# Moving weight splits and routing operations in VectorE's order of a gated cross-attention and expert kernel

## The chip, the core and the metric

One core of one Trainium2 chip. The time is that of one execution on the device, in microseconds (us). The kernel is written instruction by instruction: each engine has a program of its own, in a fixed order, and the engines meet at semaphores.

## The reference, cut to what matters

4096 rows (64 sequences of 64) of 128 numbers go through a gated attention against a context of the same shape, and then through a layer of 8 experts of which each row uses one.

```
q, k, v = rope(LN(x) @ Wq.T + bq), rope(ctx @ Wk.T + bk), ctx @ Wv.T + bv      # 16 heads of 8
x = x + tanh(g_xattn) * (softmax(q k / sqrt(8)) v @ Wo.T + bo)
z = LN(x)
logits = z @ Wr + br                                                        # 128 to 8
idx, gate = argmax(logits), the largest of softmax(logits)
x = x + tanh(g_ffn) * gate * (gelu(z @ W1[idx] + b1[idx]) @ W2[idx] + b2[idx])
```

## The kernel before

A tile is 128 rows (two sequences), so there are T = 32 tiles. All engines run through the same numbered steps (`pipeline(step)`), and in step i each works on tiles of different ages: on VectorE the query scaling of tile i, the key copy of tile i - 1, the row maxima of tile i - 2, the normalised output of tile i - 5 and the sum with the residual of tile i - 6. Nothing schedules this: the order of an engine's work in a step is the order of the code in its function `step`.

The engines' shares in an attention step are these.

- TensorE: query products (L748), key and value products (L749, L750), transposes of the stacked halves (L763), weighted values (L775), transpose of the normalised output (L788), scores (L799), transposed scores less the maxima (L814, L817), transposes of the output (L825), output product (L830, L831), transpose of the maxima (L839).
- VectorE: reciprocal and normalised output (L1132, L1135), query scaling `qk` (L1161), sum with the residual `x_all` (L1167), key copy `kT` (L1177), statistics of a coming tile (L865, L867, up to step 23), row maxima `mx` (L1195), casts of the rotated queries and keys `stk` (L1212, L1213), statistics of the finished rows (L1218, L1220).
- ScalarE: exponent `pr` (L569), maxima copy (L575), key scaling (L589), query copy `qT` (L606), output copies `oT`, `onT` (L612, L617), value copies `vx` (L627).
- GpSimd: subtraction for the low halves `stk` (L507), scatter of routed rows (L493), and the rotation (rope) in three operations (L522, L524, L528), which needs the scaled queries and keys of the same step. VectorE's casts need the rotated ones.
- The DMA queue loads the key blocks that the scores read, and the experts' weights.

Between these stands work of two other kinds. **Weight splits:** `EXPERT_AT` is step 4 + 3e for expert e. Two steps after, VectorE takes the last row off the first layer's weights (L1145, `w_f<-w_f,w_r`, 128 x 512), then ScalarE casts them to 16 bits (L601, `w_h`), and a step later VectorE makes the low half from both (L1149, `w_l<-w_f,w_h`). There are 8 of each, in steps 6 to 28. **Routing:** the tiles are routed in 5 groups (`GROUPS`). A group whose last tile is finished in step n is at `GROUP_AT` n = 11, 19, 27, 33, 37. VectorE adds epsilon in step n, and then works on the group in steps n + 2 (`before`: scaled L960, logits L970, max L976), n + 3 (`after`: difference L982, candidate L988, first L996, one-hot L1002, part L1008, count L1015) and n + 4 (`third`: exponent sum L1045, place L1026, destination L1033, index L1039, reciprocal L1051, gate L1057). Between count and place TensorE makes the ranks of the rows (`rank_of`, L662 to L669), by sums of one-hot rows. For the first three groups they go into PSUM bank 6, beside the query product's output, and for the last two into bank 1; they are issued in step n + 4, ahead of the query product in the first three groups.

After the attention, from step F0 = 35 on, 39 tiles of sorted rows pass through the experts: normalised and transposed, first layer (L710 to L712), gelu, second layer (L726, L728), final sum `fin` (L1260) and a scatter to the output (L540).

The lines of VectorE's step that say which group is at which stage, and where the weights' turn comes:

```
before, after, third = (GROUP_AT.get(i - n) for n in (2, 3, 4))
if after is not None:
    route_dif(after)
if third is not None:
    route_sum(third)
if i - 2 in EXPERT_AT:
```

## Time and profile before

| | |
|---|---|
| median of 3 runs | 324.67 us (323.63 to 325.26) |
| the profiled execution | 324.98 us |
| its span, first to last instruction | 323.2 us |
| busy: TensorE, its weight loads | 247.2 us (76%), 204.9 us (63%) |
| busy: VectorE, ScalarE, GpSimd | 196.2 (61%), 158.0 (49%), 182.6 us (57%) |
| mean granted TensorE clock | 0.928 of 2.4 GHz |
| DMA | 26.64 MB, 82 GB/s |

The median is what counts. The profile comes from one execution, with a time stamp for each instruction, so durations and waits are read in that one. Idle time in brackets behind a row is that of the engine just before the instruction, with what ended it. A blocked instruction, which was issued but can't go on, shows as a long one and not as idle time.

### The profile page before, as it was taken

To read this page: it belongs to the slowest core of one execution; us is meant where nothing else is said; L and a number is where in the kernel's file an instruction comes from. 1 tells how busy PE (TensorE), PEld (TensorE's weight loads), DVE (VectorE), ACT (ScalarE), POOL (GpSimd) and SP (SyncE) were. 2 spreads that over 40 slices of the span, in tenths; PEclk is the share of its full clock that TensorE was granted. 3 is DMA by queue.
4 is the path that set the end of the run, shared out by engine and by line. 5 is a ranking of instruction groups with operands and counts; after the bars stand their busy time and mean duration, and the time that the engine had idled before them with its cause. 6 is when DMAs were issued, how large, how long until landed. Compare 5 with 4: busy or idle time off the path is not lost.

```text
span 323.2 us, 10769 instructions
## 1 busy us (share of the span) xinstructions
PE 247.2 (76%) x3593; PEld 204.9 (63%) x3593; DVE 196.2 (61%) x680; ACT 158.0 (49%) x481; POOL 182.6 (57%) x222
## 2 busy tenths in 40 slices
PE   1458898888898978788878537694559898998970
PEld 1246677676677756577656426593559697996960
DVE  5457787888988889877797506652723333243420
ACT  1244667677676847676766203431523343343420
POOL 6475647476577886687867750046254434353450
PEclk9999999999999999999999755967897999799996
DMA  7612646254636342515111212201232212111100
GB/s 223 187 20 37 180 107 181 61 163 123 160 88 157 101 123 44 126 40 139 35 38 39 63 54 60 52 21 62 61 95 64 77 57 61 43 53 44 33 26 0
DMA packets 58537, 26.64 MB, mean 82 GB/s; under 512 B 38608, under 2 KB 53989, under 8 KB 58484
## 3 DMA queue, kind: packets, MB, share of 16 engines
q1 hardware_dynamic: 55204, 20.15, 25.1%
q0 software_dynamic: 2272, 4.46, 4.3%
q10 hardware_dynamic: 1008, 1.34, 1.4%
q8 instruction: 31, 0.51, 0.6%
q14 instruction: 22, 0.18, 0.2%
HBM read 16.69 MB, written 5.51 MB: 69 GB/s over the span
## 4 chain that ended last, share of the span: by engine, by line
PE 33%; DVE 19%; POOL 19%; issue 14%; another core or an unknown queue 5%; ACT 3%; POOLq 2%; DMA 1%; SPq 0%; DVEq 0%; ACTq 0%
PE ps L728 12%; POOL rot L528 5%; POOL rot L522 5%; POOL rot_s L524 5%; PE ps L710 3%; PE ps L712 3%; PE ps L711 3%; PE ps L763 2%; DVE qk L1161 2%; POOLq L91 2%; DVE mx L1195 2%; POOL stk L507 2%; DVE stk L1212 2%; PE ps L775 2%
## 5 line engine op out<-in xcount | busy, mean ns | idle before, releaser
L540 POOL DMA_INDIRECT out<-fin,got x39 | 37.9, 972 | 50.5 <-DVE fin L1260 35.9
L1195 DVE TENSOR_REDUCE mx<-ps 128x16 f16<-128x1024 f32 x32 | 39.1, 1221 | 22.1 <-PE ps L799 11.5
L728 PE MATMUL ps<-w_f,hT 128*128 x312 | 49.0, 305 | 0.0
L1260 DVE SCALAR_TENSOR_TENSOR fin<-ps,got 128x128 f32<-128x128 f32 x39 | 13.7, 351 | 57.2 <-PE ps L728 38.6
L728 PEld LDWEIGHTS ps<-w_f,hT 128*128 128x128 f32 x312 | 42.0, 209 | 1.1 <-issue 0.2
L522 POOL TENSOR_TENSOR rot<-qk,cf 128x256 f32<-128x256 f32 x32 | 23.4, 731 | 31.0 <-ACT qk L589 22.5
L493 POOL DMA_INDIRECT rows<-x_all,dest_i x32 | 34.0, 1062 | 8.2 <-issue 5.1
L817 PE MATMUL ps<-qT,kbd 128*128 128x64 f16 x512 | 34.8, 196 | 3.8 <-issue 3.8
L638 ACT ACTIVATE hT<-ps 128x512 f32<-128x512 f32 x39 | 23.3, 598 | 29.3 <-PE ps L712 24.0
L814 PE MATMUL ps<-mxT,ch 128*128 128x128 f16 x256 | 34.7, 225 | 2.0 <-issue 2.0
L569 ACT ACTIVATE pr<-ps 128x1024 f32<-128x1024 f32 x32 | 32.8, 1024 | 4.2 <-PE ps L817 3.3
L817 PEld LDWEIGHTS ps<-qT,kbd 128*128 128x128 f16 x512 | 32.0, 100 | 3.5 <-issue 3.5
L763 PE MATMUL ps<-ch,stk 128*128 128x128 f16 x256 | 20.7, 227 | 15.1 <-POOL stk L507 13.5
L710 PE MATMUL ps<-gT,w_h 128*128 128x128 f16 x156 | 31.7, 233 | 0.0
L711 PE MATMUL ps<-gT,w_h 128*128 128x128 f16 x156 | 31.6, 232 | 0.0
L712 PE MATMUL ps<-gT,w_l 128*128 128x128 f16 x156 | 31.5, 232 | 0.0
L763 PEld LDWEIGHTS ps<-ch,stk 128*128 128x128 f16 x256 | 16.0, 101 | 24.4 <-issue 14.1
L814 PEld LDWEIGHTS ps<-mxT,ch 128*128 128x128 f16 x256 | 25.5, 100 | 9.3 <-issue 9.2
L585 ACT ACTIVATE x_all<-ps 128x8 f32<-128x8 f32 x32 | 5.7, 178 | 51.7 <-DVE qk L1161 49.9
L507 POOL TENSOR_TENSOR stk<-rot,stk 128x256 f16<-128x256 f32 x32 | 21.4, 669 | 16.4 <-DVE stk L1213 16.4
L580 ACT ACTIVATE gT<-ps 128x128 f16<-128x128 f32 x39 | 10.8, 277 | 37.5 <-PE ps L697 24.0
L627 ACT ACTIVATE vx<-ps 64x64 f32<-64x64 f32 x128 | 27.9, 218 | 2.3
(160 smaller groups left out, 638.9 us busy)
## 6 DMA issues: line engine op xcount, KB each, us to landing
kbd<-kT SPq DMA_DIRECT2D x128, 32.0 KB
got<-rows SPq DMA_DIRECT2D x39, 72.0 KB
w_f<-in_W_rows SPq DMA_DIRECT2D x8, 256.0 KB, 2.9
w_r<-in_W_last_row SPq DMA_DIRECT2D x8, 256.0 KB, 3.1
w_f<-in_L_ffn_W SPq DMA_DIRECT2D x8, 256.0 KB
x_all<-in_x SPq DMA_DIRECT2D x3, 512.0 KB, 4.7
xt_all<-in_x_t SPq DMA_DIRECT2D x3, 512.0 KB, 4.4
ct_all<-in_ctx SPq DMA_DIRECT2D x3, 512.0 KB, 4.4
```

What stands on the lines that cost most here:

```text
L493: pool.indirect_dma_start(out=rows, out_offset=bass.IndirectOffsetOnAxis(ap=dest_i[:, t:t + 1], axis=0), in_=x_all[:, t, :], in_offset=Non ...
L522: pool.tensor_tensor(rot[:, par, :].rearrange("p (h d) -> p h d", d=HD), f, over_h(cos_t, 2 * H), ALU.mult).then_inc(rope1, 1)
L540: pool.indirect_dma_start(out=out_d, out_offset=bass.IndirectOffsetOnAxis(ap=got_i[:, u % GOT, R_ID:R_ID + 1], axis=0), in_=fin[:, u % FRI ...
L569: act.activation(pr[:, t % 2, :, :, :].rearrange("p j b q -> p (j b q)"), ps_st[:, :], ACT.Exp, scale=SCALE).then_inc(p_rdy, 1)
L710: pe.matmul(o, w_h, gT[:, par, 0, :], start=True, stop=False)
L711: pe.matmul(o, w_h, gT[:, par, 1, :], start=False, stop=False)
L712: mm = pe.matmul(o, w_l, gT[:, par, 0, :], start=False, stop=True)
L728: mm = pe.matmul(o, hT[:, par, c, :], w2_f[:, bass.ds(e, 1), c, :].rearrange("p o n -> p (o n)"), start=False, stop=(c == FC - 1))
L763: mm = pe.transpose(ps_stk[:, c:c + P], stk[:, par, first + a * P:first + a * P + P], ident_h)
L814: pe.matmul(ps_st[:, P * j:P * j + P], sel_h[:, j, :], mxT[:, par, :], start=True, stop=False)
L817: mm = pe.matmul(ps_st[:, c:c + S], kbd[:, s, j % 2, 2 * (j // 2) + b, :, :].rearrange("p h k -> p (h k)"), qT[:, s, j // 2, S * b:S * b + ...
L1195: dve.tensor_reduce(mx[:, t % 2, 0:H], ps_s[:, :].rearrange("p (h k) -> p h k", k=S), AX.X, ALU.max).then_inc(mx_done, 1)
```

## The change

VectorE's order in a step is written anew, and the ranks get another place. In words:

- The query scaling and the residual sum come right after the normalised output. The exponent sum, the two weight split operations and the place operation, which stood ahead of the query scaling, go behind it.
- Between the key copy and the row maxima now stand all of a group's operations of that step. The `before` stage has the difference in addition, so a group's difference is made one step earlier. The place operation alone stands ahead of the key copy. Nothing of the routing but the variance is left behind the maxima.
- The two weight splits stand between the key copy and the row maxima too.
- The ranks (`rank_of`) of all groups are made in step n + 3 instead of n + 4, after the transposes of the output, in bank 4, which the transpose of the normalised output and the output product use. They wait for the copy of that transpose. The next step's transpose into the bank waits until VectorE has read the ranks.

The order of GpSimd, ScalarE and of the DMA queue is the same.

```diff
-        ps_rank = [bank[6 if g <= EARLY else 1][:, 136:136 + 8 * NE] for g in range(len(GROUPS))]
-        ps_end = [bank[n][:, 208:208 + NE] for n in (6, 1)]
+        ps_rank = bank[4][:, 272:272 + 8 * NE]
+        ps_end = bank[4][:, 344:344 + NE]
...
@@ tensor, rank_of
-                if g > EARLY:
-                    pe.wait_ge(p_rdy, T)
-                    pe.wait_ge(g_read, g)
+                wait(pe, g_read, g)
...
@@ tensor, step
-                    if GROUP_AT.get(i - 4, len(GROUPS)) <= EARLY:
-                        rank_of(GROUP_AT[i - 4])
                     pe.matmul(ps_qx, xt_all[:, t, :], wqx[:, :], start=True, stop=True)
...
-                if GROUP_AT.get(i - 4, -1) > EARLY:
-                    rank_of(GROUP_AT[i - 4])
...
                     wait(pe, x2_done, t)
+                    if i - 4 in GROUP_AT:
+                        pe.wait_ge(g_read, GROUP_AT[i - 4] + 1)
                     pe.transpose(ps_onT, on[:, t % 2, :], ident).then_inc(onT_done, 1)
...
                     mm.then_inc(oT_done, 1)
+                if i - 3 in GROUP_AT:
+                    if live(i - 5):
+                        pe.wait_ge(onT_ev, i - 4)
+                    else:
+                        pe.wait_ge(x2_done, T)
+                    rank_of(GROUP_AT[i - 3])
...
@@ vector, step, after the normalised output
+                t = i
+                if live(t):
...
+                    dve.scalar_tensor_tensor(out=qk[:, t % 2, 0:D], in0=ps_q, scalar=rstd[:, t, :], in1=bq_bc[:, :],
+                                             op0=ALU.mult, op1=ALU.add).then_inc(qe_ev, 1)
+                t = i - 6
...
+                    dve.tensor_tensor(x_all[:, t, 0:QX], ps_op, x_all[:, t, 0:QX], ALU.add).then_inc(x2_done, 1)
+                if third is not None:
+                    route_place(third)
+                t = i - 1
...
+                    dve.tensor_copy(kT[:, t % 2, :, :].rearrange("p a n -> p (a n)"), ps_stk[:, NA * P:2 * NA * P]
+                                    ).then_inc(kT_ev, 1)
+                if before is not None:
+                    route_scaled(before)
                 if after is not None:
-                    route_dif(after)
+                    route_cand(after)
                 if third is not None:
                     route_sum(third)
+                    route_dest(third)
+                for t in STATS_AT.get(i, ()):
+                    stats_of(t)
+                if before is not None:
+                    route_logits(before)
+                if after is not None:
+                    route_first(after)
+                if third is not None:
+                    route_recip(third)
+                    route_index(third)
                 if i - 2 in EXPERT_AT:
...
                 if before is not None:
+                    route_max(before)
                 if after is not None:
                     route_onehot(after)
                 if third is not None:
+                    route_gates(third)
+                if before is not None:
+                    route_dif(before)
+                if after is not None:
+                    route_part(after)
+                    route_count(after)
                 t = i - 2
                 if live(t):
                     dve.wait_ge(s_done, t + 1)
                     wait(dve, mxT_done, t - 1)
                     dve.tensor_reduce(mx[:, t % 2, 0:H], ps_s[:, :].rearrange("p (h k) -> p h k", k=S), AX.X, ALU.max
                                       ).then_inc(mx_done, 1)
```

VectorE's order around the query scaling of step 12, before (`on` the normalised output, `w_f` the weights, `qk` the scaling, `kT` the key copy, `st`, `mv` the statistics, `mx` the maxima, `stk` the casts):

```order
L1135 TENSOR_TENSOR on<-ps,rden 128x128
L1145 TENSOR_TENSOR w_f<-w_f,w_r 128x512
L1161 SCALAR_TENSOR_TENSOR qk<-ps,rstd,bq_bc 128x128
L1167 TENSOR_TENSOR x_all<-ps,x_all 128x136
L1177 COPY kT<-ps 128x512
L865 BN_STATS st<-x_all 128x6
L867 BN_AGGR mv<-st 128x2
L1195 TENSOR_REDUCE mx<-ps 128x16
L1212 CAST stk<-rot 128x16x16
```

The same stretch now:

```order
L1137 TENSOR_TENSOR on<-ps,rden 128x128
L1147 SCALAR_TENSOR_TENSOR qk<-ps,rstd,bq_bc 128x128
L1153 TENSOR_TENSOR x_all<-ps,x_all 128x136
L1161 COPY kT<-ps 128x512
L867 BN_STATS st<-x_all 128x6
L869 BN_AGGR mv<-st 128x2
L1182 TENSOR_TENSOR w_f<-w_f,w_r 128x512
L1203 TENSOR_REDUCE mx<-ps 128x16
L1214 CAST stk<-rot 128x16x16
```

The subtraction `w_f` moved from ahead of the scaling to just ahead of the maxima. The low half `w_l` does the same in the steps that have it.

VectorE in step 13, where the first group is in its `before` stage and a low half is due, from the normalised output to the scaling of step 14, before:

```order
L1135 TENSOR_TENSOR on<-ps,rden 128x128
L1149 SCALAR_TENSOR_TENSOR w_l<-w_f,w_h 128x512
L1161 SCALAR_TENSOR_TENSOR qk<-ps,rstd,bq_bc 128x128
L1167 TENSOR_TENSOR x_all<-ps,x_all 128x136
L1177 COPY kT<-ps 128x512
L960 TENSOR_TENSOR logit<-x_all 128x48
L865 BN_STATS st<-x_all 128x6
L867 BN_AGGR mv<-st 128x2
L970 TENSOR_TENSOR logit<-logit,br_bc 128x48
L1195 TENSOR_REDUCE mx<-ps 128x16
L976 TENSOR_REDUCE lmax<-logit 128x6
```

Now:

```order
L1137 TENSOR_TENSOR on<-ps,rden 128x128
L1147 SCALAR_TENSOR_TENSOR qk<-ps,rstd,bq_bc 128x128
L1153 TENSOR_TENSOR x_all<-ps,x_all 128x136
L1161 COPY kT<-ps 128x512
L962 TENSOR_TENSOR logit<-x_all 128x48
L867 BN_STATS st<-x_all 128x6
L869 BN_AGGR mv<-st 128x2
L972 TENSOR_TENSOR logit<-logit,br_bc 128x48
L1186 SCALAR_TENSOR_TENSOR w_l<-w_f,w_h 128x512
L978 TENSOR_REDUCE lmax<-logit 128x6
L984 TENSOR_TENSOR ldif<-logit,lmax 128x48
L1203 TENSOR_REDUCE mx<-ps 128x16
```

The low half, the maximum of the logits and the difference (which stood in the next step, ahead of its scaling) are now ahead of the maxima.

TensorE at the end of step 14 and the start of step 15, before (`ps<-oh,ch` and `ps<-ohsum,ch` are the ranks, `wqx` the query product, `c_h` and `wo_x` the output product, `mx` the transpose of the maxima):

```order
L831 MATMUL ps<-wo_x,onT 128x136
L839 MATMUL ps<-ch,mx 128x128
L662 MATMUL ps<-oh,ch 128x48
L665 MATMUL ps<-oh,ch 128x40
L665 MATMUL ps<-oh,ch 128x32
L665 MATMUL ps<-oh,ch 128x24
L665 MATMUL ps<-oh,ch 128x16
L665 MATMUL ps<-oh,ch 128x8
L667 MATMUL ps<-ohsum,ch 128x48
L748 MATMUL ps<-wqx,xt_all 128x136
```

Now:

```order
L821 MATMUL ps<-cf,oT 128x128 x2
L660 MATMUL ps<-oh,ch 128x48
L663 MATMUL ps<-oh,ch 128x40
L663 MATMUL ps<-oh,ch 128x32
L663 MATMUL ps<-oh,ch 128x24
L663 MATMUL ps<-oh,ch 128x16
L663 MATMUL ps<-oh,ch 128x8
L665 MATMUL ps<-ohsum,ch 128x48
L832 MATMUL ps<-c_h,ch 128x136
L833 MATMUL ps<-wo_x,onT 128x136
L841 MATMUL ps<-ch,mx 128x128
L744 MATMUL ps<-wqx,xt_all 128x136
```

The ranks moved from between the transpose of the maxima and the query product to ahead of the output product of the step before.

## Rows read from the trace of the kernel before

**Rows 1.** The chain of waits, its shares of the span by line.

```profile
by line: issue 13.8%; PE ps L728 11.6%; another core or an unknown queue 5.2%; POOL rot L528 5.2%; POOL rot L522 5.2%; POOL rot_s L524 4.9%; PE ps L710 3.1%; PE ps L712 2.8%; PE ps L711 2.7%; PE ps L763 2.0%; DVE qk L1161 1.9%; POOLq L91 1.
```

**Rows 2.** VectorE's query scaling as a line: duration ns min/median/max, first and last start.

```profile
L1161 DVE SCALAR_TENSOR_TENSOR qk<-ps,rstd,bq_bc x32: 337/344/352, 11.6 to 175.5; 128x128 f32<-128x128 f32 x32
```

**Rows 3.** Timeline, VectorE, steps 9 and 10: start, duration, operation, idle before.

```profile
57.97 0.34 DVE L1161 SCALAR_TENSOR_TENSOR qk<-ps,rstd,bq_bc 128x128 f32<-128x128 f32 x1
...
62.48 0.68 DVE L1149 SCALAR_TENSOR_TENSOR w_l<-w_f,w_h 128x512 f16<-128x512 f32 x1
63.08 0.34 DVE L1161 SCALAR_TENSOR_TENSOR qk<-ps,rstd,bq_bc 128x128 f32<-128x128 f32 x1
...
63.55 0.42 DVE L1177 COPY kT<-ps 128x512 f16<-128x512 f16 x1
...
64.20 0.18 DVE L867 BATCH_NORM_AGGREGATE mv<-st 128x2 f32<-128x6 f32 x1
64.68 1.23 DVE L1195 TENSOR_REDUCE mx<-ps 128x16 f16<-128x1024 f32 x1 [0.30 <-PE ps L799]
66.28 0.29 DVE L1212 CAST stk<-rot 128x256 f16<-128x256 f32 x1 [0.38 <-POOL rot L528]
...
67.59 0.34 DVE L1161 SCALAR_TENSOR_TENSOR qk<-ps,rstd,bq_bc 128x128 f32<-128x128 f32 x1
```

**Rows 4.** Timeline, GpSimd, step 10: the three rotations.

```profile
64.03 0.72 POOL L522 TENSOR_TENSOR rot<-qk,cf 128x256 f32<-128x256 f32 x1 [1.61 <-ACT qk L589]
64.71 0.72 POOL L524 TENSOR_TENSOR rot_s<-qk,cf 128x256 f32<-128x256 f32 x1
65.52 0.73 POOL L528 TENSOR_TENSOR rot<-rot,rot_s 128x256 f32<-128x256 f32 x1
```

**Rows 5.** Timeline, TensorE, steps 9 and 10: products for the next step.

```profile
61.20 0.50 PE L748 MATMUL ps<-wqx,xt_all 128*128 128x136 f32 x2
...
61.97 0.22 PE L750 MATMUL ps<-bk_h,ch 128*128 128x128 f16 x1
...
66.14 0.45 PE L748 MATMUL ps<-wqx,xt_all 128*128 128x136 f32 x2
```

**Rows 6.** Timeline, ScalarE, step 9: weight cast and value copies.

```profile
58.78 0.63 ACT L601 ACTIVATE w_h<-w_f 128x512 f16<-128x512 f32 x1
...
60.20 0.95 ACT L627 ACTIVATE vx<-ps 64x64 f32<-64x64 f32 x4
```

**Rows 7.** VectorE beside GpSimd: timeline of steps 5 and 14, then a line's durations (ns).

```profile
41.23 0.67 POOL L507 TENSOR_TENSOR stk<-rot,stk 128x256 f16<-128x256 f32 x1 [0.61 <-DVE stk L1213]
41.56 0.89 DVE L1145 TENSOR_TENSOR w_f<-w_f,w_r 128x512 f32<-128x512 f32 x1
84.08 0.73 POOL L522 TENSOR_TENSOR rot<-qk,cf 128x256 f32<-128x256 f32 x1 [1.13 <-ACT qk L589]
84.58 0.29 DVE L1002 TENSOR_TENSOR oh<-cand,cmax 128x48 f16<-128x48 f32 x1
L1002 DVE TENSOR_TENSOR oh<-cand,cmax x5: 191/291/657, 84.6 to 223.3; 128x48 f16<-128x48 f32 x2, 128x64 f16<-128x64 f32 x2, 128x32 f16<-128x32 f32 x1
```

**Rows 8.** The row scatter as a line: duration ns min/median/max.

```profile
L493 POOL DMA_INDIRECT rows<-x_all,dest_i x32: 969/970/1467, 94.3 to 237.9; - x32
```

**Rows 9.** Timeline, VectorE: logit scaling of step 29, and scalings of steps 13 and 14.

```profile
164.17 1.69 DVE L960 TENSOR_TENSOR logit<-x_all 128x64 f32<-128x64 f32 x1
...
78.50 0.34 DVE L1161 SCALAR_TENSOR_TENSOR qk<-ps,rstd,bq_bc 128x128 f32<-128x128 f32 x1
...
83.14 0.34 DVE L1161 SCALAR_TENSOR_TENSOR qk<-ps,rstd,bq_bc 128x128 f32<-128x128 f32 x1
```

**Rows 10.** Timeline, first group's ranks on TensorE, and the scaling behind them.

```profile
87.79 0.18 PE L662 MATMUL ps<-oh,ch 128*128 128x48 f16 x1 [1.06 <-DVE ohsum L1015]
...
89.09 0.34 DVE L1161 SCALAR_TENSOR_TENSOR qk<-ps,rstd,bq_bc 128x128 f32<-128x128 f32 x1
```

**Rows 11.** Timeline, VectorE, the longest wait behind the last attention step.

```profile
193.41 1.22 DVE L1195 TENSOR_REDUCE mx<-ps 128x16 f16<-128x1024 f32 x1 [10.53 <-remote]
```

More of the change, by code:

```diff
@@ L668, in rank_of @@
                 if g in (EARLY, len(GROUPS) - 1):
[L669 removed]
+                    mm = pe.matmul(ps_end, ones_h, ohsum[:, g + 1, :], start=True, stop=True)
                 mm.then_inc(g_rank, 1)
@@ L1137, in step @@
                                       ALU.mult).then_inc(on_done, 1)
-                if after is not None:
-                    route_dif(after)
-                if third is not None:
-                    route_sum(third)
-                if i - 2 in EXPERT_AT:
-                    e = EXPERT_AT[i - 2]
-                    dve.wait_ge(s_w1ld[e % 2], 32 * (e // 2 + 1))
-                    dve.tensor_tensor(w1_f[:, e % 2, :], w1_f[:, e % 2, :], w1_r[:, e % 2, :], ALU.subtract).then_inc(s_w1c, 1)
-                if i - 3 in EXPERT_AT:
-                    e = EXPERT_AT[i - 3]
-                    dve.wait_ge(s_w1hi, e + 1)
-                    dve.scalar_tensor_tensor(out=w1_l[:, e, :], in0=w1_f[:, e % 2, :], scalar=W_SCALE,
-                                             in1=w1_h[:, e, :], op0=ALU.mult, op1=ALU.subtract).then_inc(s_w1lo, 1)
-                if third is not None:
-                    wait(dve, qkv_done, i + 1 if live(i) else 0)
-                    route_place(third)
                 t = i
@@ L1167, in step @@
                     dve.tensor_tensor(x_all[:, t, 0:QX], ps_op, x_all[:, t, 0:QX], ALU.add).then_inc(x2_done, 1)
-                if after is not None:
-                    route_cand(after)
                 if third is not None:
-                    route_dest(third)
+                    route_place(third)
                 t = i - 1
@@ L1181, in step @@
                 if after is not None:
-                    route_first(after)
+                    route_cand(after)
+                if third is not None:
+                    route_sum(third)
+                    route_dest(third)
                 for t in STATS_AT.get(i, ()):
@@ L1196, in step @@
                                       ).then_inc(mx_done, 1)
-                if before is not None:
-                    route_max(before)
-                if after is not None:
-                    route_part(after)
-                if third is not None:
-                    route_recip(third)
                 t = i
@@ L1238, in step @@
                     route_var(GROUP_AT[i])
-                if after is not None:
-                    route_count(after)
-                if third is not None:
-                    route_gates(third)
                 if i == F0 - 4:
```

19 lines of the change are left out of this document (13 added, 6 removed).

## The prediction

> **What bounds the kernel now.** I read the chain of waits first [rows 1]. Its largest named share is TensorE's second layer of the experts, which the change doesn't touch; then come GpSimd's three rotation operations, 5% of the span each. So the attention pipeline hangs on GpSimd, and on the small pieces of other engines between its turns. Then the query scaling of VectorE, which runs once a step [rows 2]: 32 times, from 11.6 to 175.5 us. The 31 steps between take 163.9 us, and the change lies almost wholly inside them. Below, q is the start of that operation, and times in a step are counted from it.
>
> A step without expert or routing work lasts 4.51 us, from 63.08 to 67.59 [rows 3]. In it the key copy begins at 0.47 and the statistics end at 1.30; the row maxima start at 1.60. GpSimd's rotations run from 0.95 to 1.67, 1.63 to 2.35 and 2.44 to 3.17 [rows 4]. VectorE waits 0.38 us for the last one, casts at 3.20, and reaches the next q 1.31 us after that. It idles 0.30 + 0.38 us between the key copy and the cast. That is the room into which the change moves work.
>
> Two more limits follow from the rows. From the start of the maxima, 64.68, to the first product of the next query, 66.14, are 1.46 us [rows 3, 5], and that group of products takes 0.99 (61.20 to 62.19) before q can start: a step lasts at least the start of the maxima plus 2.45. And the query product waits for ScalarE's value copies. With a weight cast, ScalarE takes 2.37 us from that cast, 58.78, to the end of the value copies, 61.15; the product starts 0.05 later [rows 5, 6].
>
> **The change part by part.**
>
> *Weight splits taken from ahead of q.* There are 16; one lasts 0.68 us and the next operation starts 0.60 after it did [rows 3]. The step from 57.97 to 63.08 has one ahead of its end and lasts 5.11 [rows 3]. Where VectorE's loop sets the step, each gives back 0.60.
>
> *Weight splits put beside the rotations.* In the new place a split is issued at about 1.33, within the rotation that runs from 0.95 to 1.67. VectorE operations that read two operands of SBUF do not run there. The one-hot comparison issued at 84.58 lasts 0.29, where 0.19 is its shortest, and ends 0.06 after the rotation [rows 7]. The first weight split met GpSimd's subtraction: it took 0.89 instead of 0.68 and ended 0.54 after the subtraction's end at 41.90 [rows 7]. The other way round, row scatters on GpSimd last 0.97 us and up to 1.47 [rows 8], and the long ones are those issued just after a split. So whoever comes first holds the other up, and a split needs 0.55 us in which GpSimd stands. The Trainium skill has this in "SBUF — State Buffer", section "Who interferes with whom": a VectorE instruction with two SBUF inputs contends with a GpSimd instruction that reads SBUF, and one of them blocks fully. The trace agrees, with the 0.89 above. By that rule the idle 0.68 us are no room for a split; taken as free room, they would give the faster rival's time below.
>
> No row has a weight split between two rotations, so I bound it. From below: it gets in when the first rotation ends, as five of the six small operations did that were waiting then (the bias addition twice, the one-hot comparison three times, at 0.29 to 0.66 us [rows 7]). From above: the logit scaling at 164.17 lasted 1.69, over two rotations [rows 9]. I take the first, as what most of the rows did, and keep the second.
>
> *A step with the low half:* split from 1.67 to 2.25, maxima from 2.25, the second and third rotation 0.6 later, cast at 3.81, next q at 5.12. It was 5.11. Nothing is gained.
>
> *A step with the subtraction of the last row:* the same on VectorE, but ScalarE's cast of these weights waits for it, and behind that cast stand the query copy, two output copies and the value copies. Before, the subtraction was done ahead of q. Now it ends at 2.30; the cast starts at 2.36, the value copies end at 4.73, the products run from 4.78 to 5.77: a step of 5.75 for 5.11, so +0.64.
>
> *Routing operations.* They take three steps for each of the groups in the attention: scaling, bias, maximum and difference in 13, 21, 29; candidate, maximum, comparison, part and count in 14, 22, 30; place, sums, reciprocal, index and gate in 15, 23, 31. All now stand ahead of the maxima, at 0.15 to 0.25 us each, and each with two SBUF inputs waits out a rotation. Step 13 lasted 4.63, from 78.50 to 83.14 [rows 9]. Now the bias addition ends with the first rotation, the low half gets in at 2.37 and ends at 2.97, the third rotation runs until 3.70, the difference waits for it, the maxima start at 3.78: 3.78 + 2.45 = 6.23, and only 0.60 comes back in the step before. In the same way step 14 gets 6.15 for 5.96, and step 15, where the subtraction slips to the second gap and ScalarE follows it, 6.47 for 5.25.
>
> *Ranks a step earlier, in the output product's bank.* TensorE idled 1.06 us for the count and began the ranks at 87.79, with the query products behind them, so that q came at 89.09 [rows 10]. Of that step's 5.96 the subtraction is 0.60 and the ranks about 0.35. Now they run while VectorE takes the maxima. In return the read of the ranks, 0.2 us, stands between the output sum and the key copy, and the transpose into the bank waits for it with the scores behind. The 0.30 of idle time ahead of the maxima hides that; uncovered it would be 0.2 in three steps.
>
> *The sum*, in threes of steps, worked by these rules for both kernels so that the same errors stand on both sides:
> steps 5 to 7: +1.55 (the first subtraction loses 0.42 ahead of q, but the key copy is late there and the split meets the second gap: 6.47 for 5.11);
> 8 to 10: +0.65, and 17 to 19: +0.70, the plain kind;
> 11 to 13, 14 to 16, 20 to 22, with group work: +1.55, +1.55, +1.15;
> 23 to 28: -0.05, since from 24 on there are no statistics, splits come before the first rotation, and the scatters, free of the 0.5 us that splits cost them, give back what the rotations lose;
> 29 and 30: -0.95, the ranks.
> Together +6.15. After the attention nothing changes its kind. The long wait of the maxima, 10.53 us until 193.41 [rows 11], lies behind nine row scatters that start from the last attention step, so I let it move with that step. The profiled execution becomes 324.98 + 6.15 = 331.1; it lies 0.31 above the median of 324.67, so the median should be **330.8**.
>
> **The rivals.**
>
> *The splits get in only in the second gap*, like the logit scaling [rows 9]. Maxima start at 2.97, the steps last 5.42 and 6.47 instead of 5.12 and 5.75: +1.02 in each plain triple, nothing where they are there already, +3.0 in all by the same rules: 333.8. For it: one waiting operation was passed over. Against it: five were not. If they are passed over until the third rotation ends, it is 342; no row shows that.
>
> *Faster: a long operation shares the port.* If a split runs its 0.68 us beside a rotation, as the statistics do [rows 3, 4], the maxima start at 1.93, under the 2.06 that a 4.51 us step allows. Each low half then gains 0.60, and each subtraction gains 0.60 ahead of q and costs 0.9 through ScalarE (1.99 + 0.06 + 2.37 + 0.05 + 0.99 = 5.46 for 4.51); with the ranks the rules give -2.65, so 322. It decides at a split of 0.68 beside rotations of 0.73. Against it stands the 0.89.
>
> *Little or no difference.* My three group triples stand on margins of 0.05 us between the issue of an operation and the end of a rotation; if they lose half, and late steps hide more, +1 to +2 is left.
>
> **How the numbers follow.** The forecast's case gets 0.52, its own range 328 to 333; the second gap 0.22 (332.5 to 336), the third 0.04; the faster rival 0.12 (320 to 323); little or none 0.10 (323.5 to 327). A measurement tells 0.5%, 1.6 us, from no change. Faster by more 0.12, within 0.07, slower 0.81. The range 326 to 336 leaves out the faster rival and the third gap.
>
> **What would show it.** In the changed kernel's trace: splits issued about 1.3 after q that last 0.9 to 1.0 us (second gap: 1.6), a second rotation of about 1.3 us; a step near 5.75 where ScalarE's weight cast starts with the end of the subtraction and TensorE waits for the value copies; step 13 over 6; scatters in the attention near 1.0; no idle time for the count ahead of the ranks; the last scaling at about 181.5 instead of 175.5. I am wrong if splits last 0.68 and rotations 0.73 there, or if the last scaling comes by 176, and wrong in size if the steps with group work last under 5.5.

## The result, and the profile after

| | before | after |
|---|---|---|
| median | 324.97 us (4 runs) | 335.44 us (4 runs, 334.62 to 336.48) |
| the profiled execution, its span | 324.98, 323.2 us | 335.75, 334.0 us |
| last query scaling, step 31 | 175.5 us | 186.9 us |
| from there to the end of the span | 147.7 us | 147.1 us |

The change makes the kernel slower: the ratio is 1.032 (95% interval 1.028 to 1.035). That is within the forecast range of 326 to 336, by 0.6 us, and 4.6 us above the 330.8 forecast: outside the 328 to 333 of the forecast's own case and inside the 332.5 to 336 of the rival with the second gap. Up to the last query scaling 11.4 us are lost, and 0.6 come back behind it.

From the page of the kernel after: the span, the busy times, and the chain that ended last, by line.

```profile
span 334.0 us, 10768 instructions
...
PE 253.3 (76%) x3593; PEld 204.5 (61%) x3593; DVE 208.2 (62%) x680; ACT 161.2 (48%) x481; POOL 187.0 (56%) x222
...
PE ps L726 9%; DVE mx L1203 4%; PE ps L759 3%; PE ps L708 3%; DVE w_f L1182 3%; DVE kT L1161 2%; PE ps L710 2%; PE ps L709 2%; POOL rot L528 2%; PE ps L745 2%; ACT vx L627 2%; POOL rot_s L524 2%; POOL rot L522 2%; ACT pr L569 2%
```

VectorE runs as many instructions as before and is busy 12.0 us longer (208.2 for 196.2), since operations that are issued and blocked count as busy. In the chain the rotations fell from 5% each [rows 1] to 2%. The subtraction `w_f` (L1182) is new in it, with the row maxima right behind it.

The subtraction (with who waited for it: us, times), the low half, GpSimd's second rotation and the scatter as lines of the kernel after: duration ns min/median/max, first and last start.

```profile
L1182 DVE TENSOR_TENSOR w_f<-w_f,w_r x8: 658/1129/2168, 43.4 to 163.2; 128x512 f32<-128x512 f32 x8
...
  ACT w_h L601: 14.6, 8
...
L1186 DVE SCALAR_TENSOR_TENSOR w_l<-w_f,w_h x8: 678/793/1198, 49.9 to 170.7; 128x512 f16<-128x512 f32 x8
...
L524 POOL TENSOR_TENSOR rot_s<-qk,cf x32: 718/728/1208, 13.2 to 188.7; 128x256 f32<-128x256 f32 x32
...
L493 POOL DMA_INDIRECT rows<-x_all,dest_i x32: 966/976/1187, 97.8 to 248.7; - x32
```

Splits last up to 2.17 us, and ScalarE's weight cast waits 14.6 us for the eight subtractions. The scatters behave as I wrote: 1.19 at most for 1.47 [rows 8]. So the scatters no longer lose time to splits, but nothing came back for it.

The plain step with a subtraction, step 9: timeline of the kernel after (start, duration, operation, idle before), VectorE, then GpSimd and ScalarE.

```profile
57.94 0.34 DVE L1147 SCALAR_TENSOR_TENSOR qk<-ps,rstd,bq_bc 128x128 f32<-128x128 f32 x1
...
59.15 1.00 DVE L1182 TENSOR_TENSOR w_f<-w_f,w_r 128x512 f32<-128x512 f32 x1
60.07 1.21 DVE L1203 TENSOR_REDUCE mx<-ps 128x16 f16<-128x1024 f32 x1
...
63.69 0.35 DVE L1147 SCALAR_TENSOR_TENSOR qk<-ps,rstd,bq_bc 128x128 f32<-128x128 f32 x1 [0.72 <-PE ps L746]
```

```profile
58.88 0.72 POOL L522 TENSOR_TENSOR rot<-qk,cf 128x256 f32<-128x256 f32 x1 [1.52 <-ACT qk L589]
59.56 1.17 POOL L524 TENSOR_TENSOR rot_s<-qk,cf 128x256 f32<-128x256 f32 x1
```

```profile
60.18 0.63 ACT L601 ACTIVATE w_h<-w_f 128x512 f16<-128x512 f32 x1 [1.27 <-DVE w_f L1182]
```

The split is issued 1.21 after q, lasts 1.00 instead of 0.68, and ends 0.55 after the first rotation; the second rotation lasts 1.17 instead of 0.72. ScalarE's cast starts with the split's end, and the next q waits 0.72 us for TensorE. The step is 63.69 - 57.94 = 5.75, for 5.11 before. This is the mechanism of the forecast, complete; that the number agrees to the hundredth is luck, as said further down.

Late in the attention it looks otherwise. Step 24, same views:

```profile
144.94 0.35 DVE L1147 SCALAR_TENSOR_TENSOR qk<-ps,rstd,bq_bc 128x128 f32<-128x128 f32 x1
...
145.95 2.17 DVE L1182 TENSOR_TENSOR w_f<-w_f,w_r 128x512 f32<-128x512 f32 x1
148.04 1.21 DVE L1203 TENSOR_REDUCE mx<-ps 128x16 f16<-128x1024 f32 x1
...
152.03 0.35 DVE L1147 SCALAR_TENSOR_TENSOR qk<-ps,rstd,bq_bc 128x128 f32<-128x128 f32 x1 [1.37 <-PE ps L746]
```

```profile
145.05 1.06 POOL L493 DMA_INDIRECT rows<-x_all,dest_i  x1 [0.19 <-POOL stk L507]
146.14 0.74 POOL L522 TENSOR_TENSOR rot<-qk,cf 128x256 f32<-128x256 f32 x1
146.82 0.73 POOL L524 TENSOR_TENSOR rot_s<-qk,cf 128x256 f32<-128x256 f32 x1
147.64 1.06 POOL L528 TENSOR_TENSOR rot<-rot,rot_s 128x256 f32<-128x256 f32 x1
```

```profile
148.15 0.63 ACT L601 ACTIVATE w_h<-w_f 128x512 f16<-128x512 f32 x1 [2.24 <-DVE w_f L1182]
```

The split was issued during a row scatter, 0.16 us before that ended. It stayed blocked through the first and the second rotation and ran in the second gap. ScalarE waited 2.24 us. The step lasts 7.09 for 5.21. Step 27 does the same (split 2.09, step 7.13 for 5.52).

There is a second loss in it. TensorE waited for ScalarE's output copy, and soon after its granted clock fell. TensorE in step 24, then two windows with their length, busy times and clock (the number before the DMA share):

```profile
149.59 0.44 PE L821 MATMUL ps<-cf,oT 128*128 128x128 f32 x2 [1.60 <-ACT oT L612]
...
150.91 0.91 PE L745 MATMUL ps<-wkv,ct_all 128*128 128x256 f32 x2
```

```profile
148.00:149.50 1.50, 0.00 (x0) 0.00 (x0) 1.50 (x4) 1.35 (x4) 0.70 (x1) 1.00 0.28 47
...
151.20:154.40 3.20, 3.14 (x46) 1.99 (x46) 1.77 (x4) 2.03 (x7) 1.79 (x3) 0.50 0.09 28
```

TensorE had nothing for 1.60 us; soon after, the clock stood at 0.50, its lower level of 1.2 GHz, for over 3 us, then came back. The key and value product took 0.91 there and takes 0.59 at full clock. By step the clock is 0.93, 0.78, 0.92 and 0.80 in steps 24, 25, 27 and 28, and 1.00 in every other step from 5 to 30. Before the change it is 1.00 in all of them. The Trainium skill ("TensorE: Matmul & The Clock Gate", Part 1) says that the clock has these two levels and falls after the engine has been idle; the trace agrees on the levels, with 0.50 and 1.00. That this wait brought the clock down is not shown: in the same kernel TensorE idled as long in steps 15 and 21, 1.53 and 1.66 us, and kept 1.00. In step 21:

```profile
130.60 0.44 PE L821 MATMUL ps<-cf,oT 128*128 128x128 f32 x2 [1.66 <-ACT oT L612]
```

Where the 11.4 us came from, in the triples of the forecast:

| steps | forecast | measured |
|---|---|---|
| 5 to 7 | +1.55 | +0.95 |
| 8 to 10 | +0.65 | +0.46 |
| 11 to 13 | +1.55 | +1.47 |
| 14 to 16 | +1.55 | +1.47 |
| 17 to 19 | +0.70 | +1.30 |
| 20 to 22 | +1.15 | +1.02 |
| 23 to 28 | -0.05 | **+4.98** |
| 29, 30 | -0.95 | -0.26 |
| sum | +6.15 | +11.39 |

The term of steps 23 to 28 was 5.0 us too low, of the 5.2 us that are missing. The others were off by up to 0.7 us each way and cancel to 0.2.

### The profile page after: what moved, and what is told of

The parts are those of the page before. It is cut to its first block, busy times and chain, and to the rows that moved or that the text cites. A ratio compares the mean times of both kernels' runs of the same rounds, so it can differ in the third digit from the quotient of the medians.

```text
span 334.0 us, 10768 instructions
## 1 busy us (share of the span) xinstructions
PE 253.3 (76%) x3593; PEld 204.5 (61%) x3593; DVE 208.2 (62%) x680; ACT 161.2 (48%) x481; POOL 187.0 (56%) x222
## 4 chain that ended last, share of the span: by engine, by line
PE 31%; DVE 26%; issue 13%; POOL 9%; another core or an unknown queue 8%; ACT 8%; DMA 1%; POOLq 0%; SPq 0%; DVEq 0%; ACTq 0%
PE ps L726 9%; DVE mx L1203 4%; PE ps L759 3%; PE ps L708 3%; DVE w_f L1182 3%; DVE kT L1161 2%; PE ps L710 2%; PE ps L709 2%; POOL rot L528 2%; PE ps L745 2%; ACT vx L627 2%; POOL rot_s L524 2%; POOL rot L522 2%; ACT pr L569 2%
## 5 line engine op out<-in xcount | busy, mean ns | idle before, releaser
L1203 DVE TENSOR_REDUCE mx<-ps 128x16 f16<-128x1024 f32 x32 | 38.9, 1217 | 18.5 <-remote 10.6
L726 PE MATMUL ps<-w_f,hT 128*128 x312 | 48.2, 302 | 0.0
L726 PEld LDWEIGHTS ps<-w_f,hT 128*128 128x128 f32 x312 | 41.2, 206 | 1.1 <-issue 0.2
L522 POOL TENSOR_TENSOR rot<-qk,cf 128x256 f32<-128x256 f32 x32 | 23.3, 729 | 28.2 <-ACT qk L589 20.1
L493 POOL DMA_INDIRECT rows<-x_all,dest_i x32 | 32.0, 1001 | 7.9 <-issue 5.5
L528 POOL TENSOR_TENSOR rot<-rot,rot_s 128x256 f32<-128x256 f32 x32 | 27.3, 854 | 2.5
L759 PE MATMUL ps<-ch,stk 128*128 128x128 f16 x256 | 21.5, 233 | 8.9 <-POOL stk L507 3.6
```

What stands on the lines that cost most here:

```text
L528: pool.tensor_tensor(rot[:, par, :], rot[:, par, :], rot_s[:, par, :], ALU.add).then_inc(rope_done, 1)
L726: mm = pe.matmul(o, hT[:, par, c, :], w2_f[:, bass.ds(e, 1), c, :].rearrange("p o n -> p (o n)"), start=False, stop=(c == FC - 1))
L759: mm = pe.transpose(ps_stk[:, c:c + P], stk[:, par, first + a * P:first + a * P + P], ident_h)
L1203: dve.tensor_reduce(mx[:, t % 2, 0:H], ps_s[:, :].rearrange("p (h k) -> p h k", k=S), AX.X, ALU.max).then_inc(mx_done, 1)
```

## The experiments

Most runs fell on chips where the kernel before takes 304.7 to 305.0 us and not 324.97; only the last experiment had 324.97 beside it. So I took the kernel before once more there, with its profile.

**before_again**: the kernel before, no edit.

> The kernel before, with a profile on this chip, to see where the 20 us between the chips lie. If they lie in the waits behind the attention (10.5 us of the maxima and two others of 5 and 6.4 us), the last query scaling starts at 175.5 as before and the rest is shorter; if the chip is faster throughout, every step is shorter.

Measured: 305.28 us, span 303.5. Its steps agree with those of the first profile to within 0.03 us, but for step 30 (6.15 for 6.24), and the last scaling is at 175.5 in both. The 20 us lie behind it. VectorE's waits in the first profile, then here (total, times, longest):

```profile
DVE fin L1260 <- remote: 14.0, 3, 6.4
...
DVE mx L1195 <- remote: 10.5, 1, 10.5
```

```profile
DVE fin L1260 <- PE ps L728: 44.9, 37, 2.5
DVE mx L1195 <- PE ps L799: 12.8, 21, 2.0
```

The waits put down to "remote", the 10.53 us of [rows 11] among them, don't exist on the other chips. The kernel after has them as well on the first chip, at 10.6 us for 10.5, so they are no matter of the change. I therefore read each experiment against the kernel before on its own chip, as a difference; expectations in absolute numbers near 325 mean that difference too.

**changed_again**: the changed kernel on such a chip.

> The changed kernel itself, beside the kernel before, on the chip of these studies, on which the kernel before takes 304.7 to 305.0 us instead of 324.97. If the loss lies in the attention steps alone, the difference is the same 10.5 us or a little more (11.4 by the last query scaling), so 315 to 317; if a part of it is due to the waits behind the attention, it differs by more than 2 us from that.

Measured: 316.21 for 305.03 us, +11.2, ratio 1.036 (1.030 to 1.042); last scaling at 187.1. Loss and step lengths are those of the first chip (steps to within 0.07 us), and so is the clock (0.94, 0.77, 0.92, 0.80 in steps 24, 25, 27, 28).

**splits_back**: the changed kernel with both weight splits ahead of the query scaling again, as two blocks moved up.

```diff
@@ vector, step, after the normalised output
+                if i - 2 in EXPERT_AT:
...
+                    dve.tensor_tensor(w1_f[:, e % 2, :], w1_f[:, e % 2, :], w1_r[:, e % 2, :], ALU.subtract).then_inc(s_w1c, 1)
+                if i - 3 in EXPERT_AT:
...
+                    dve.scalar_tensor_tensor(out=w1_l[:, e, :], in0=w1_f[:, e % 2, :], scalar=W_SCALE,
+                                             in1=w1_h[:, e, :], op0=ALU.mult, op1=ALU.subtract).then_inc(s_w1lo, 1)
@@ ahead of the query scaling; the same two blocks taken out ahead of the row maxima
```

> The changed kernel with both weight split operations ahead of the query scaling again; ranks and routing stay as changed. Theory 1 (a VectorE operation with two SBUF inputs waits for GpSimd's rotations, and ScalarE's weight cast waits for the subtraction): the splits carry most of the loss; left are the routing operations that wait out rotations in nine steps, less the ranks: 326 to 328. Theory 2 (routing and ranks carry the loss): stays above 332. Theory 3 (VectorE has simply too much work ahead of the maxima, no lock): each split was worth no more than its 0.6 us, 331 or more.

**splits_only**: the other half, the kernel before with only these two blocks moved to just ahead of the row maxima.

> The kernel before with the two split operations alone moved to just ahead of the row maxima; ranks and routing as before. Theory 1: 331 to 333, splits of 0.9 to 2.2 us beside the rotations, steps 24 and 27 near 7 us. Theory 2: 325. Theory 3: under 328, splits of 0.68 us.

Measured: splits_back 306.76 for 304.71 us, +2.05 (1.002 to 1.011); splits_only 312.88, +8.2 (1.024 to 1.034). Together 10.2, near the whole 11.2. So the place of the 16 splits is worth 8.2 us when it is changed alone and 9.2 when it is taken back, three quarters to four fifths of the loss; the routing order and the ranks together cost the rest. In neither run does the clock fall between steps 5 and 31, as it does with both parts in; that may be why the two don't quite add up. In splits_only step 27 shows the blocked split of 2.08 us at full clock and lasts 6.64. Step 24, which I had expected near 7 as well, lasts 5.76: its split ran at once behind the scatter and took 0.95.

**subtraction_back**: the changed kernel with only the `w_f` block ahead of the query scaling; the low half stays ahead of the maxima.

> The changed kernel with the subtraction of the last row ahead of the query scaling again; the low half stays beside the rotations. Theory 1: the low half costs nothing in plain steps and some 0.3 to 1 us where it meets the second gap: 328 to 330; steps with the weight cast on ScalarE are 5.1 us again. Theory 3: gains the same as moving the low half back would, so half of what moving both gives.

Measured: 307.33 for 304.71 us, +2.6 (1.006 to 1.011). Taking back the subtraction alone gives 8.6 of 11.2; I had expected a loss of 3.3 to 5.3 to be left. Beside splits_back (+2.05) the eight low halves in their new place cost some 0.5 us together, which is within the intervals; in the two traces steps 5 to 30 differ by 1.4. Three of the eight are blocked (2.02, 0.85 and 2.10 us), and only VectorE's own row maxima stand behind them.

**cast_late**: the changed kernel, where ScalarE makes the weight cast behind the value copies instead of ahead of the query copy.

```diff
@@ scalar, step
-                if i - 2 in EXPERT_AT:
...
-                    act.activation(w1_h[:, e, :], w1_f[:, e % 2, :], ACT.Copy, scale=W_SCALE).then_inc(s_w1hi, 1)
...
+                if i - 2 in EXPERT_AT:
...
+                    act.activation(w1_h[:, e, :], w1_f[:, e % 2, :], ACT.Copy, scale=W_SCALE).then_inc(s_w1hi, 1)
```

> The changed kernel with ScalarE's weight cast behind its value copies, so that nothing of the step waits for the subtraction there. Theory 1: plain steps with the subtraction fall from 5.75 to about 5.15, steps 18, 24 and 27 by 1 to 1.5 us each: 329 to 331.5 in all. If ScalarE's order does not matter (VectorE or GpSimd alone set these steps): 334 or more.

Measured: 309.83 for 304.71 us, +5.1 (1.012 to 1.020). The splits block as before (1.01 in step 9). Step 9 is 4.96 instead of 5.75, steps 24 and 27 are 5.53 and 5.82, and the clock stays at 1.00. So 6.1 of the 11.2 us pass through ScalarE's queue, the part of the clock among them: the cast waits for the split, and copies that TensorE needs stand behind it. What stays are VectorE's own delay of the maxima and the moved routing operations.

**one_input**: the changed kernel with both splits replaced by reductions that read one SBUF operand.

```diff
-                    dve.tensor_tensor(w1_f[:, e % 2, :], w1_f[:, e % 2, :], w1_r[:, e % 2, :], ALU.subtract).then_inc(s_w1c, 1)
+                    dve.tensor_reduce(w1_f[:, e % 2, :], w1_f[:, e % 2, :].rearrange("p (n o) -> p n o", o=1), AX.X, ALU.max).then_inc(s_w1c, 1)
...
+                    dve.tensor_reduce(w1_l[:, e, :], w1_f[:, e % 2, :].rearrange("p (n o) -> p n o", o=1), AX.X, ALU.max).then_inc(s_w1lo, 1)
```

> The changed kernel with both split operations replaced, at their new place, by reductions over one element each: the same 128 x 512 elements and outputs, but one SBUF input. This leaves out the subtraction of the last row and the low halves of the weights. Theory 1: these operations last about the 0.68 us of a free split beside the rotations, the second rotation is 0.73 again, only ScalarE's cast chain and the routing stay: 326 to 329. Theory 3: no difference to the changed kernel, 335.

Measured: 308.87 for 305.04 us, +3.8 (1.008 to 1.020). The subtraction's place and the second rotation, as lines:

```profile
L1182 DVE TENSOR_REDUCE w_f<-w_f x8: 652/663/677, 42.9 to 156.5; 128x512 f32<-128x512 f32 x8
...
L524 POOL TENSOR_TENSOR rot_s<-qk,cf x32: 712/727/734, 13.5 to 179.5; 128x256 f32<-128x256 f32 x32
```

Same place, same size, same length, one operand fewer: nothing is blocked, neither the reductions (0.68 at most, in the low half's place as well) nor the rotation (0.73 at most). The blocking is worth 7.4 us of the 11.2.

The reductions are also another kind of operation. Two more lines tell kind and operands apart: in the kernel after, the normalised output, a TENSOR_TENSOR of which one operand is in PSUM; and in ranks_only, the epsilon added to a variance, which reads one SBUF operand and a constant.

```profile
L1137 DVE TENSOR_TENSOR on<-ps,rden x32: 291/291/292, 37.2 to 220.5; 128x128 f32<-128x128 f32 x32
L873 DVE TENSOR_SCALAR rvar<-mv x8: 169/345/702, 9.3 to 134.6; 128x4 f32<-128x4 f32 x8
```

The first never takes longer than 0.29 us, though most of them in the attention are issued while GpSimd is in a TENSOR_TENSOR. So it is not the kind TENSOR_TENSOR that blocks the splits, but that both operands are in SBUF. The second does wait, with one SBUF operand: in all five attention steps that have it, it ends 0.02 to 0.05 us behind a rotation. Two SBUF operands are thus enough to be blocked here, and not the only way to be.

Step 9 is 5.41 in one_input. The faster rival had reckoned 5.46 for it, from ScalarE's chain alone. Steps 8 and 9 take 10.44 for 11.09 before, and 0.60 of that is the low half that left the end of step 9. So even without any blocking the subtraction in this place would have gained next to nothing.

**splits_behind_sum**: the kernel before with the two blocks right behind the residual sum, before the key copy.

> The kernel before with both split operations moved to just behind the residual sum, ahead of the key copy, at about 0.47 us after the start of the query scaling, where GpSimd reads nothing until the first rotation at 0.95. Theory 1: splits of 0.68 to 0.75 us, the first rotation later by up to 0.15, the steps with a split 4.6 to 4.9 instead of 5.1 where no scatter stands ahead of the rotation: 319 to 322. Theory 3: what is ahead of the maxima counts alike wherever it stands, so as the kernel with the splits alone moved.

Measured: 301.77 for 305.04 us, ratio 0.988 (0.985 to 0.991), 3.3 us *faster* than before. VectorE in step 9, and GpSimd beside it:

```profile
56.23 0.34 DVE L1152 SCALAR_TENSOR_TENSOR qk<-ps,rstd,bq_bc 128x128 f32<-128x128 f32 x1
...
56.69 0.68 DVE L1162 TENSOR_TENSOR w_f<-w_f,w_r 128x512 f32<-128x512 f32 x1
```

```profile
57.17 0.79 POOL L522 TENSOR_TENSOR rot<-qk,cf 128x256 f32<-128x256 f32 x1 [1.52 <-ACT qk L589]
```

The split is issued 0.46 after q and is nearly through when the first rotation comes, which loses 0.07. The key copy and the statistics move into the idle time ahead of the maxima. The step lasts 4.76 for 5.11. Some steps grew all the same: 16 by 1.0, 27 by 0.7 and 22 by 0.5, which I didn't follow up. In the traces steps 5 to 30 are 1.5 us shorter together. Another 0.8 is gained in step 2, before any split: TensorE's products took 0.47 and 0.59 us there instead of 0.79 and 1.06. one_input has the same short step 2, so that part need not belong to the edit. The room was there, ahead of the rotations and not beside them.

**after_splits_behind_sum**: the changed kernel with the same move.

> The changed kernel with both split operations just behind the residual sum. Theory 1: the routing operations that wait out rotations stay, the splits' part goes and a little more: 324 to 327. Theory 3: 335.

Measured: 303.03 for 305.04 us, ratio 0.993 (0.990 to 0.996). One place of two blocks turns the change from +11.2 to -2.0, more than the -0.7 at best that I had expected. All 16 splits last 0.68 us. The median is 1.3 us above that of splits_behind_sum, but in the traces steps 5 to 30 are 1.0 us shorter than there (135.23 for 136.25); I have no cause for the 1.3.

**ranks_only**: the kernel before with the ranks as changed, and of VectorE's order only what they need (the place operation behind the residual sum, part and count ahead of the maxima).

> The kernel before with the ranks a step earlier in bank 4, the place operation behind the residual sum, part and count ahead of the maxima; splits and the other routing operations as before. Theory: steps 14, 22 and 30 lose TensorE's wait for the count, 0.4 to 0.9 us each, less 0.1 to 0.2 for part, count and place ahead of the maxima: 302.5 to 304.5. A rival: the count, with two SBUF inputs, waits out a rotation ahead of the maxima and takes the gain back: 304.5 to 305.5.

Measured: 303.37 for 305.03 us, ratio 0.993 (0.990 to 0.996). TensorE in step 14, with the ranks in a row and no idle time:

```profile
87.29 0.19 PE L660 MATMUL ps<-oh,ch 128*128 128x48 f16 x1
87.32 0.27 PE L663 MATMUL ps<-oh,ch 128*128 128x40 f16 x5
87.44 0.18 PE L665 MATMUL ps<-ohsum,ch 128*128 128x48 f16 x1
```

Against before_again steps 14, 22 and 30 fell from 5.96, 6.27 and 6.15 to 5.44, 5.16 and 4.93. But steps 15 and 23 rose from 5.25 and 5.27 to 5.83 and 5.85: their small operations now meet the rotations. In step 15:

```profile
91.39 0.70 DVE L873 TENSOR_SCALAR rvar<-mv 128x4 f32<-128x4 f32 x1
...
92.08 1.21 DVE L1199 TENSOR_REDUCE mx<-ps 128x16 f16<-128x1024 f32 x1
```

An operation of four elements a lane takes 0.70 us and the maxima stand behind it. The move of the ranks was the part of the change that pays, 1.7 us.

**ranks_and_splits_behind_sum**: both together.

> The same with the splits just behind the residual sum. If both gains are their own: the 3.3 us of the splits there and those of the ranks, 299.5 to 301. If the group steps are set by the rotations once the splits are gone, no less than the 301.8 of the splits alone.

Measured: 299.34 for 305.03 us, ratio 0.984 (0.978 to 0.989), span 296.7, last scaling at 169.3. This version is faster than both kernels. It differs from after_splits_behind_sum (303.03) in the routing order alone: with the routing left where it was, the time is 3.7 us shorter, 3.4 of them in steps 5 to 30. That is what the routing operations ahead of the maxima cost.

**scatter_behind**: the changed kernel, with GpSimd's scatters issued behind the three rotations of a step instead of ahead of them. It asks whether the scatter is why splits passed over the first gap.

```diff
@@ gpsimd, step
-                for _ in range(SCATTER_AT.get(i, 0)):
-                    scatter()
...
@@ behind the third rotation
+                for _ in range(SCATTER_AT.get(i, 0)):
+                    scatter()
```

> The changed kernel with GpSimd's row scatters of a step behind its three rotations instead of ahead of them. In the traces so far a weight split that waits for the first rotation gets in at its end, except where that rotation starts 0.03 us behind a scatter: then it waits out the second too (11 of 12 times). Theory 1b (the scatter just ahead is what does it): splits of 2.1 us in steps 24 and 27 and of 1.66 in step 18 become 1.0 to 1.4 with a second rotation of 1.2, these steps fall to about 5.8, and the scatter costs 0.2 to 0.4 in the steps where it now holds up GpSimd's subtraction: 312 to 316 against 316.2, with the steps as the proof, not the sum. If it is the place in the program or the phase of the engines, the splits of steps 18, 24 and 27 stay at 1.6 to 2.1 us.

Measured: 334.33 for 324.97 us, ratio 1.030 (1.025 to 1.035). Step 24 again, VectorE and GpSimd (whose rotations are now L520, L522 and L526):

```profile
145.75 0.35 DVE L1147 SCALAR_TENSOR_TENSOR qk<-ps,rstd,bq_bc 128x128 f32<-128x128 f32 x1
...
146.76 1.21 DVE L1182 TENSOR_TENSOR w_f<-w_f,w_r 128x512 f32<-128x512 f32 x1
...
151.52 0.35 DVE L1147 SCALAR_TENSOR_TENSOR qk<-ps,rstd,bq_bc 128x128 f32<-128x128 f32 x1 [0.73 <-PE ps L746]
```

```profile
146.70 0.73 POOL L520 TENSOR_TENSOR rot<-qk,cf 128x256 f32<-128x256 f32 x1 [1.02 <-ACT qk L589]
147.38 1.18 POOL L522 TENSOR_TENSOR rot_s<-qk,cf 128x256 f32<-128x256 f32 x1
```

The split is issued 1.01 after q, as in the changed kernel, but into a rotation that follows nothing directly. It gets in at the first gap and lasts 1.21. The splits of steps 18, 24 and 27 fall from 1.66, 2.17 and 2.09 to 0.66, 1.21 and 1.03, these steps from 6.64, 7.09 and 7.13 to 5.78, 5.77 and 5.76, and steps 23 to 28 together from +4.98 to +2.77. The clock stays at 1.00 in them, which is part of the gain. So taking the scatter away from ahead of the first rotation ends the passing over in these three steps. It is not the scatter as such: in step 28 of this run a low half is passed over behind another GpSimd operation.

```profile
169.01 2.01 DVE L1186 SCALAR_TENSOR_TENSOR w_l<-w_f,w_h 128x512 f16<-128x512 f32 x1
```

```profile
167.41 1.68 POOL L479 TENSOR_TENSOR x_all<-rvar,cf 128x8 f32<-128x8 f32 x1
169.06 0.72 POOL L520 TENSOR_TENSOR rot<-qk,cf 128x256 f32<-128x256 f32 x1
```

The gain is mostly eaten, since scatters behind the rotations hold up the next step: step 20 grows from 5.70 to 6.89. Step 13 grew from 6.04 to 6.55. No scatter had moved before it; the granted clock in it is 0.74.

## Why the prediction was right or wrong

Some steps in numbers, us:

| step | before | forecast | after | one_input | cast_late | scatter_behind | splits_behind_sum |
|---|---|---|---|---|---|---|---|
| 6 | 5.10 | 6.47 | 5.80 | 5.80 | 5.23 | 5.80 | 5.20 |
| 9 | 5.11 | 5.75 | 5.75 | 5.41 | 4.96 | 5.76 | 4.76 |
| 10 | 4.51 | 5.12 | 5.27 | 4.88 | 4.96 | 5.27 | 4.81 |
| 13 | 4.63 | 6.23 | 6.04 | 5.73 | 6.02 | 6.55 | 5.07 |
| 14 | 5.96 | 6.15 | 5.53 | 5.54 | 5.54 | 5.54 | 5.96 |
| 15 | 5.25 | 6.47 | 6.67 | 6.67 | 6.07 | 6.67 | 5.29 |
| 18 | 5.16 | | 6.64 | 5.64 | 5.46 | 5.78 | 4.70 |
| 24 | 5.21 | | 7.09 | 5.24 | 5.53 | 5.77 | 5.14 |
| 27 | 5.52 | | 7.13 | 5.24 | 5.82 | 5.76 | 6.18 |

**Held by luck: the range.** The measured 335.44 is 0.6 us inside the range, and the range reaches to 336 only for the rival with the second gap, which I gave 0.22. But that rival's mechanism, the second gap in every plain triple for +1.02 each, is not what happened either: the triple 8 to 10 measured +0.46.

**Right: the mechanism in most steps.** Splits block against rotations, for a reason shown by one_input; ScalarE's cast passes the delay on to TensorE, shown by cast_late; a step comes to 5.75, step 13 to over 6. The exact 5.75 is luck: the terms of the forecast add up to 4.78 + 0.99 = 5.77; in the trace the cast starts at 2.24 and not at 2.36, and from the first product of the next query to q are 1.09 us and not 0.99. The faster rival (322) failed at the point it named: splits of 0.68 and rotations of 0.73 beside each other don't occur, except where one operand is taken away.

**Right: the group triples**, +3.96 for the forecast +4.25 over steps 11 to 16 and 20 to 22. Inside them errors cancel: step 14 is 0.62 shorter than forecast and step 13 by 0.19, and step 15 is 0.20 longer. In step 14 the ranks gave 0.52 by ranks_only where I had counted 0.35; the rest of the 0.62 I can't place.

**Wrong: steps 23 to 28, the -0.05.** I wrote that from 24 on "splits come before the first rotation", and credited the freed scatters. The split is in fact issued before that rotation, 1.0 after q, but while the scatter of that step is still running; it doesn't start when the scatter ends, and waits out two rotations. That is the wait of the rival with the second gap (2.17 us for its 1.6), in a place where I had counted none; my case and the rival were both true, each in other steps. The scatters did get short, and nothing came back for it: what they did here was to stand directly ahead of the first rotation. Of the +4.98, by the nearest steps at full clock:

- Steps 24 and 27: +1.88 and +1.61. The same step with a split of 2.08 at full clock lasts 6.64 (splits_only, step 27). So the wait and ScalarE's chain make up to 1.4 and 1.1, the clock some 0.45 and 0.49.
- Steps 25 and 28, the low half: +0.96 and +0.94. Without the clock's fall they last 5.04 and 4.96 (splits_only), so the clock makes 0.49 in each. The rest is the key copy and the scores, which come late behind a step that ended with TensorE.
- Steps 23 and 26: +0.24 and -0.65.

The clock thus makes about 1.9 us of the 4.98, a term that the forecast didn't have at all. These 1.9 come from comparing steps in different kernels; I made no run that keeps the wait and fills TensorE's idle 1.6 us, and whether the wait brought the clock down stays open.

**Wrong in size: the low half**, 5.12. Steps 7 and 10 last 5.34 and 5.27. (In the triple 8 to 10 step 8 makes up for it: 5.04 for 5.98, where I had counted 0.60 for the split gone from its end.) The key copy starts 0.98 after q and not 0.47, for TensorE is late from the step before. VectorE in step 10 of the kernel after:

```profile
64.67 0.42 DVE L1161 COPY kT<-ps 128x512 f16<-128x512 f16 x1 [0.42 <-PE ps L759]
...
65.43 1.18 DVE L1186 SCALAR_TENSOR_TENSOR w_l<-w_f,w_h 128x512 f16<-128x512 f32 x1
66.53 1.21 DVE L1203 TENSOR_REDUCE mx<-ps 128x16 f16<-128x1024 f32 x1
```

So the low half, issued 1.74 after q, meets the second gap. I had reckoned with a late key copy in step 6 only, where it was too large (6.47 for 5.80).

**Wrong in size: 17 to 19**, +1.30 for +0.70. I took it for the plain kind; in step 18 a scatter stands ahead of the rotations and the split lasts 1.66.

**Wrong in size: 29 and 30**, -0.26 for -0.95. It is the same wait again, on a routing operation. VectorE, then TensorE in step 30 of the kernel after:

```profile
181.60 1.62 DVE L990 SCALAR_TENSOR_TENSOR cand<-ldif,cf 128x64 f32<-128x64 f32 x1
```

```profile
184.78 0.19 PE L660 MATMUL ps<-oh,ch 128*128 128x64 f16 x1 [0.88 <-DVE ohsum L1017]
```

The candidate is issued 0.08 us before a scatter ends and waits out two rotations, so the count comes late, and TensorE idles 0.88 us for it ahead of the ranks; in step 22 it is 1.02. My sign "no idle time for the count" held in step 14 alone. In ranks_only, where candidate and one-hot keep their order, it holds in all three, and step 30 lasts 4.93 for 6.29 here.

**Right: behind the attention nothing changes**, -0.6 us. The long wait moved along with the last step on the first chip, as said, and is missing on others.

## What to carry to other kernels

Idle time of an engine is room for an operation only if its operands don't meet another engine's: look in the trace at what runs beside it, and move the work to where the other engine stands. Here 0.7 us further ahead in the same step turned +11.2 into -2.0. Before moving an operation behind the start of a step's chain, follow who waits for its result (here a cast in ScalarE's queue ahead of four copies) and what that leaves idle. A sum over many steps needs its late, irregular ones worked out singly: one term given as "about nothing" held nearly the whole error, while the others cancelled.

## What the runs showed of the hardware that I had not expected

- **Who gets in between two rotations.** An operation with two SBUF operands, waiting when the first rotation ends, gets in between it and the next: the splits end about 0.55 us after that (step 9). Where the first rotation followed another GpSimd operation directly, within 0.04 us (a row scatter, once the small operation L479), it mostly waited out the second rotation too: 2.17, 2.09, 2.08 and 2.01 us, and 1.66 where it was issued in the rotation itself (step 18). Not always: in step 12 of the kernel after the rotation follows L479 directly and the split still gets in at the first gap (1.03), as does the low half in step 25 of splits_only behind a scatter (0.99). One split was issued 0.28 us before the end of a scatter, in step 24 of splits_only, and ran at once when it ended, ahead of the rotation; those passed over were issued 0.16 us and less before. VectorE's split of step 12 in the kernel after and that one of splits_only are shown below. What decides between them is open. The Trainium skill ("SBUF — State Buffer", "Who interferes with whom") says that whoever issues first holds the ports and the other blocks fully. The block is as it says; by issue alone the order in these rows would be another.

```profile
75.37 1.03 DVE L1182 TENSOR_TENSOR w_f<-w_f,w_r 128x512 f32<-128x512 f32 x1
```

```profile
145.88 0.95 DVE L1185 TENSOR_TENSOR w_f<-w_f,w_r 128x512 f32<-128x512 f32 x1
```

- **The clock in the middle of a busy stretch.** TensorE idled 1.60 us (step 24) and 1.52 us (step 27), and its clock went to half for over 3 us each time, in both profiles of the changed kernel. With 1.53 and 1.66 us in steps 15 and 21 of the same kernel, and 1.51 in step 27 of splits_only, it did not. In scatter_behind it fell in step 13, where no idle stretch since step 5 had been over 1.01 us. So one idle stretch doesn't tell whether the clock will fall. Where it fell, it cost some 0.5 us in that step and again in the next (0.5 in step 13).
- **The chip.** The same kernel takes 324.97 us on one chip and 305.0 on others, at equal step lengths in the attention. The difference is waits of 6 to 10 us behind bursts of row scatters, of which the profile names no releaser on the core. I didn't try to find their cause.
